# Attention with row maxima: of every three heads, two get their maxima from one VectorE instruction over two PSUM banks

## What is computed

```
qk = jnp.einsum('bdm,bdn->bmn', qh, kh) * scale
sm = jax.nn.softmax(qk, axis=-1)
ret = jnp.einsum('bmn,bcn->bcm', sm, vh)
```

## Time and profile before

| | |
|---|---|
| runs | 1290.80, 1291.47, 1293.65 us; median 1291.47 us |
| span of the profiled execution, first to last instruction | 1274.6 us |
| what lies around the span: median less span | 16.9 us |
| mean granted TensorE clock | 0.929 of full speed |
| PE busy | 1100.8 us (86%) |
| VectorE busy | 674.0 us (53%) |
| ACT busy | 640.8 us (50%) |
| L959, the maxima | 256 instructions, 160.0 us, 682 ns each |

### The profile page before, as it was taken

The page is one execution under the profiler, slowest core; times in us unless marked ns, Lnnn a source line. Parts: engine busy times, 40 slices in busy tenths (PEclk is TensorE's granted clock), DMA queues, the critical chain, the costliest instruction groups (busy, mean ns, idle before and its releaser), DMA issues. The chain is left out here.

```text
span 1274.6 us, 19803 instructions
## 1 busy us (share of the span) xinstructions
PE 1100.8 (86%) x6973; PEld 799.6 (63%) x6974; DVE 674.0 (53%) x1388; ACT 640.8 (50%) x1016; POOL 524.5 (41%) x587
## 2 busy tenths in 40 slices
PE   4999622699699978998799999999967699999998
PEld 3545311444388865554578888888633478888887
DVE  5768578631653347785753333333577873333333
ACT  4557558489543334776334334443283454334443
POOL 5145700001246632123256656666401035666664
PEclk8789966899899998999799999999989889999999
DMA  5863130368223305431133353333100014333332
GB/s 162 244 191 125 52 115 1 84 181 193 77 96 115 112 29 160 147 116 46 53 120 115 115 177 110 111 111 106 37 9 1 1 40 145 115 113 107 111 110 69
DMA packets 65942, 131.40 MB, mean 103 GB/s; under 512 B 9307, under 2 KB 33051, under 8 KB 65366
## 3 DMA queue, kind: packets, MB, share of 16 engines
q1 hardware_dynamic: 62470, 123.10, 32.1%
q10 hardware_dynamic: 3120, 5.64, 1.4%
q0 software_dynamic: 288, 1.84, 0.4%
HBM read 114.51 MB, written 15.45 MB: 102 GB/s over the span
## 5 line engine op out<-in xcount | busy, mean ns | idle before, releaser
L1506 POOL TENSOR_TENSOR f_hid<-f_gated,f_coef 128x512 f32<-128x512 f32 x152 | 220.6, 1453 | 166.6 <-DVE f_gated L1538 157.0
L1538 DVE TENSOR_TENSOR f_gated<-f_act_g,f_p_u 128x512 f32<-128x512 f32 x152 | 104.2, 687 | 262.2 <-PE f_p_u L1322 245.6
L828 ACT ACTIVATE a_probs<-a_p_sc 128x1024 f32<-128x1024 f32 x192 | 188.9, 1020 | 27.4 <-PE a_p_sc L730 19.6
L1434 ACT ACTIVATE f_hid_hi<-f_hid 128x512 fp32r<-128x512 f32 x152 | 96.2, 633 | 203.8 <-POOL f_hid L1506 203.8
L959 DVE TENSOR_REDUCE a_maxes<-a_p_max 128x2 f32<-128x512 f32 x256 | 160.0, 682 | 41.6 <-PE a_p_max L697 41.4
L1542 DVE TENSOR_TENSOR f_hid_lo<-f_hid,f_hid_hi 128x512 fp32r<-128x512 f32 x152 | 112.6, 741 | 127.8 <-ACT f_hid_hi L1434 126.5
L1429 ACT ACTIVATE f_act_g<-f_p_g 128x512 f32<-128x512 f32 x152 | 90.4, 597 | 152.7 <-PE f_p_g L1322 148.5
L730 PE MATMUL a_p_sc<-a_q,a_k 75*128 75x256 bf16 (+1 forms) x768 | 117.8, 282 | 9.8 <-ACT a_probs L828 5.1
L1335 PE MATMUL f_p_y<-f_hid_hi,f_down_hi 128*128 128x512 f32 x292 | 114.0, 390 | 0.0
L1335 PE MATMUL f_p_y<-f_hid_hi,f_down_lo 128*128 128x512 f32 x292 | 113.7, 389 | 0.0
L1335 PE MATMUL f_p_y<-f_hid_lo,f_down_hi 128*128 128x512 f32 x292 | 113.7, 389 | 0.0
(11 more groups left out here) (309 smaller groups left out, 1706.5 us busy)
## 6 DMA issues: line engine op xcount, KB each, us to landing
f_w<-in_w SPq DMA_DIRECT2D x76, 384.0 KB, 3.5
f_coef<-coef SPq DMA_DIRECT2D x49, 512.0 KB, 3.7
a_q<-q_parts SPq DMA_DIRECT2D x48, 288.0 KB
a_k<-k_plain SPq DMA_DIRECT2D x96, 96.0 KB
outs<-a_out SPq DMA_DIRECT2D x48, 128.0 KB, 1.7
a_whole<-outs SPq DMA_DIRECT2D x48, 128.0 KB, 2.6
q_parts<-a_q_part SPq DMA_DIRECT2D x48, 96.0 KB, 3.6
a_k<-k_unit SPq DMA_DIRECT2D x24, 192.0 KB
```

The costliest lines, as they stand in the source:

```text
L828: nc.scalar.activation(probs[b % 2][:, 2 * pair:2 * pair + 2, :, :].rearrange("p h t d -> p h (t d)"), p_sc[pair % 2][:], ACT.Exp, scale=s ...
L1434: nc.scalar.activation(hid_hi[slot(t, 2)][c][:], hid[c][:], ACT.Copy).then_inc(hid_hi_done, 1)
L1506: nc.gpsimd.tensor_tensor(hid[c][:], gated[c][:], coef[slot(t, 2)][:, c * 512:(c + 1) * 512], ALU.mult).then_inc(hid_done, 1)
L1538: nc.vector.tensor_tensor(gated[c][:], act_g[c][:], p_u[c][:], ALU.mult).then_inc(gated_done, 1)
```

## The change

`take_max(n)` looks at n % 3, which is the bank. Where the bank is 0 and the head isn't the last of its batch, one instruction reads banks 0 and 1 and writes the maxima of heads n and n + 1. It waits for both heads' scores, and adds 2 to `max_taken` when it is done. The call for head n + 1 then does nothing. A head in bank 2 goes alone as before, and so do head 7 in bank 0 and the head 0 that follows it in bank 1, because a pair would cross from one batch to the next.

```diff
                 def take_max(n):
                     b, h = n // HEADS, n % HEADS
-                    dve.wait_ge(max_scored, n + 1)
+                    both = n % 3 == 0 and h < HEADS - 1
+                    if n % 3 == 1 and h > 0:
+                        return
+                    count = 2 if both else 1
+                    dve.wait_ge(max_scored, n + count)
                     if h == 0 and b >= 3:
                         dve.wait_ge(neg_split, b - 2)
-                    nc.vector.tensor_reduce(maxes[b % 3][:, :, h],
-                                            p_max[:, n % 3, :].rearrange("p (t d) -> p t d", t=NK),
-                                            axis=AX.X, op=ALU.max, negate=True).then_inc(max_taken, 1)
+                    nc.vector.tensor_reduce(maxes[b % 3][:, :, h:h + count].rearrange("p t h -> p h t"),
+                                            p_max[:, n % 3:n % 3 + count, :].rearrange("p n (t d) -> p n t d", t=NK),
+                                            axis=AX.X, op=ALU.max, negate=True).then_inc(max_taken, count)
```

## The result

The changed kernel took 1308.21 us (median of 4 runs, 1302.02 to 1313.03), the kernel before in the same comparison 1291.13 us; ratio 1.0134, 95% interval 1.0086 to 1.0183. By the medians the change makes the kernel slower by 17 us in the first comparison and by 20 in the second, by the ratios by 17 and 19. Forecast were 1308.0 us and a loss of 16.5.

The account below looks back on a forecast made before the run. It took the bound to be a loop of PE's matmuls, three VectorE instructions, head 5 and PE's remaining step. Layer 2's 9.8 and layer 0's 6.7 us made 16.5, giving 1308.0 us, 1.3% slower; range 1299 to 1321.

Parts of the forecast that it names:

- A pair costs 1.21 us: VectorE's maxima: one instruction over two banks takes 1.21 us, the next starts 1.14 after it, saving 0.07 per pair.
- The three kinds of step: 6.96, 7.09, 7.13: Attention steps with inversions, b % 3 = 1, 2, 0: PE waits make them 6.96, 7.09, 7.13 us instead of 6.52.
- Steps without inversions, 20.46 for three: Batches 4 to 6 of an attention: three steps take 20.46 us against 18.45, a loss of 2.0 us.
- Eight steps with inversions, 4.3 us: Batches 7 to 14 of each attention: eight steps lose 0.54 us each, 4.3 us per attention.
- The start, 2.0 us: Layer 2, first matmul to first scores: 12.2 us instead of 10.18, 2.0 lost; batch 2's turn 0.5 later again.
- Batch 15, 0.7 us: Last batch of each attention: 0.7 us lost, 0.6 from batch 14's late turn and a little for its own.
- Layer 0, 6.7 us: Layer 0's attention: 8.0 us lost, less up to 1.0 and 0.3 hidden in waits, leaving 6.7.
- The clock rival: PE's new waits drop its clock, 1.6 us per fall: 1319 us if one step in three falls, 1325 if every second; chance 0.21.
- The sum on the median: Whole kernel: predicted span 1291.1 us plus the 16.9 us by which the runs' median exceeds the profiled span, 1308.0 us.
- faster: Rival: VectorE's total work in the step counts, so 76 pairs saving 0.07 each give 5 us, 1286 us; chance 0.03.
- unchanged: Rival: the waits fall into PE's slack of 0.56 us per step, giving 1289 to 1294 us; chance 0.04.

Follow-up runs that it names:

- the second: The changed kernel timed again in more rounds against the kernel before: 1309.86 against 1289.47 us, ratio 1.0146, interval 1.0114 to 1.0178.

## Why the prediction was right, step by step

The direction, the mechanism and the size hold; the first comparison's median is 0.2 us from the forecast, which is chance, since the later one puts the loss 2 us higher. The sum is also nearer than its parts: layer 2 lost 14.2 us where the forecast had 9.8, and layer 0 lost 4.8 where it had 6.7. That the two errors partly cancel is luck.

- *A pair costs 1.21 us.* Measured 1.22 (1218 ns), 0.54 more than a single for 512 more columns, where the prediction had 0.53.
- *The three kinds of step: 6.96, 7.09, 7.13.* Measured 7.17, 7.06, 7.17. The first was 0.2 short: the pair (1,2) starts 0.50 after the matmuls that follow a turn (572.26 to 572.76), where I took 0.42, and the pair (6,7) before it was held by the inversion, so the turn came at A + 1.20 and not 1.10.
- *Steps without inversions, 20.46 for three.* Measured 20.86, 20.64, 20.84 in the three profiles (18.47 before): 2.3 us for 2.0.
- *Eight steps with inversions, 4.3 us.* Mis-sized: batches 7 to 14 took 60.15, 58.55 and 60.13 us in the three profiles of the change against 51.85 before, a mean of 7.8 more. Of this, 2.6 are falls of the clock (two, one, two times 1.57), 0.6 the kind b % 3 = 1, and 0.4 a slip in counting: batch 7's step has no inversion ahead of its head 2 and took 6.16, not 6.53.
- *The start, 2.0 us.* Measured from the first matmul (499.39) to the first scores (511.81) 12.42 in two profiles, against 10.19, 10.59 and 9.98 before: 2.2. The third profile of the change has 15.21, with the fall in it, so the mean is 3.1. The turn behind it came 7.61 after the first scores, where it had been 6.98: 0.6 for 0.5. From that turn to batch 4's first heads, a stretch partly at the low clock in both kernels, 7.61, 8.86 and 7.68 us stand against 8.22, 8.06 and 8.19: 0.1 less in the mean, where I had 0.3 more.
- *Batch 15, 0.7 us.* From its first heads to the next stage 30.9 us against 30.0 in the mean: 0.9.
- *Layer 0, 6.7 us.* Measured 4.8, within a scatter of several us. That waits for DMAs hide part of it was right in kind: PE's wait for the maxima's DMA was 1.03, 4.22 and 4.23 us before and 0.44, 1.70 and 1.61 after, 1.9 less in the mean, where I let it hide up to 1.0. The bound of 1.0 came from the one profile in which this wait was short. How much the other waits hide, three profiles on each side don't tell.
- *The clock rival, 0.21, one or more falls in three steps.* Partly true: 1 or 2 falls in 12 steps of layer 2, each at the price worked out (1.6). With the fall in the start that is about 3.5 us in the mean, which belonged in the forecast itself.
- *The sum on the median.* I wrote that the median lies 16.9 us "above that span" as if something lay around it. The later runs list both: 1305.32 us and a span of 1303.0, so 2.3 us lie around, and the rest is that the first profiled execution was a quick one (other profiles of the same kernel span 1291.7 and 1287.2). The forecast of the difference didn't need it, but some hiding read from that one profile of layer 0 is luck of that execution.
- *The rivals faster and unchanged* are out. Of the two halves of the Trainium skill's advice (Perfetto Trace Analysis, "Optimizing Scalar/DVE Operations"), the one on an engine that isn't saturated but causes bubbles elsewhere is what the runs agree with: the grouped instruction costs 0.61 us per step. The Trainium skill's figure for the fixed cost on a PSUM source (VectorE: DVE Perf Modes, "The TRN2 errata"), from which I estimated 0.125 us saved per pair, is not what the rows give: 0.68 + 0.68 - 1.22 is 0.14 in busy time, but the next instruction starts 0.60 after a single and 1.14 after a pair (583.59 to 584.73), so 0.06 in VectorE's time.

## What to carry to other kernels

Where an engine is a middle link of a ring of few buffers, its instruction's length is a latency, not a share of busy time: ask who needs the first buffer back, and when, before two reads are put into one. Check the producer's order too, because a pair whose halves are separated by other work starts late by all of that work. And look for work that needs nobody's buffer but stands on the loop: moved by two instructions, an inversion took 0.37 us out of each step of the kernel before that had it on the loop, more than half of what grouping the maxima lost; in the changed kernel, whose loop ran elsewhere, the same move took out 0.05.

## What was not expected of the hardware

Waits on PE of 0.15 and 0.73 us in one step were in some executions followed by a fall to the lower clock, while in the three profiles of the changed kernel's layer 2 the waits of 0.85 and 0.94 us, each in a step of its own, never were. In the kernel with two instructions per pair one fall came in a step with b % 3 = 0 (batch 12, 8.74 us), so this is no rule. Nor is it one in layer 0's attention: in two of the three profiles of the change a fall followed the wait of 0.93 us in batch 9 (b % 3 = 0), whose step took 8.74 and 8.73. The one step in layer 0's attention that waits for the maxima's DMA took 8.80, 12.55 and 13.21 us in three profiles of the kernel before, with waits of 1.03, 4.22 and 4.23 in it.
